# A centred output projection: the second LayerNorm without a mean of its own, and the step loop written out

## The reference

```python
x_inner, z = split(xn @ W_in.T)                 # 512 + 512 channels
x_conv = silu(causal 4-tap depthwise conv(x_inner) + conv_b)
s_C    = (x_conv @ W_x.T)[second half]          # 16 values per token
h_t    = 0.95 * h_{t-1} + x_conv_t              # along the sequence
y      = h * (s_C @ exp(B_log).T) * silu(z)
resid  = xn + y @ W_out.T
attn   = (resid - mean(resid)) * rsqrt(var(resid) + 1e-5) * ln_g + ln_b
ffn    = fp6_blocks(xn) @ fp6_blocks(weight).T + bias   # blocks of 32
out    = x + attn + ffn
```

## Time and profile before

| what | value |
|---|---|
| median of the runs shown | 272.82 us (274.34, 272.82, 272.75) |
| profiled execution, span | 272.2 us, mean granted TensorE clock 0.950 |
| profiled execution, own time | not listed apart from its span; the span is 0.62 us under the median |
| VectorE busy | 236.1 us, 87% |
| TensorE matmul busy | 217.7 us, 80% |
| GpSimd busy | 198.4 us, 73% |
| ScalarE busy | 157.8 us, 58% |

### The profile page before, as it was taken

How to read it: one execution, slowest core, us unless ns; L and a number is a source line. 1 busy time by engine, 2 the same in 40 slices (tenths; PEclk the granted TensorE clock), 3 DMA queues, 4 the chain that set the end, 5 groups by cost and what they waited for, 6 DMA issues and landing times.

```text
span 272.2 us, 3762 instructions
## 1 busy us (share of the span) xinstructions
PE 217.7 (80%) x1252; PEld 180.9 (66%) x1252; DVE 236.1 (87%) x353; ACT 157.8 (58%) x240; POOL 198.4 (73%) x127
## 2 busy tenths in 40 slices
PE   0469959789999997786999895896999988459940
PEld 0348836467898965775898763785989667359930
DVE  4799999989998999689699999689999978785374
ACT  2797773567953456858755355759737263733540
POOL 1428999999568788986586979985697959943142
PEclk9999995979999999999799999999999999959995
DMA  7963000000000000013202000000202000001204
GB/s 234 291 189 125 1 2 0 1 0 0 2 0 1 2 0 1 2 37 117 78 2 77 0 0 0 0 0 0 77 0 77 2 0 0 0 17 64 77 0 154
DMA packets 10773, 11.12 MB, mean 41 GB/s; under 512 B 648, under 2 KB 10120, under 8 KB 10760
## 3 DMA queue, kind: packets, MB, share of 16 engines
q1 hardware_dynamic: 9488, 9.96, 11.1%
q10 hardware_dynamic: 1272, 0.99, 1.3%
HBM read 6.76 MB, written 4.19 MB: 40 GB/s over the span
## 4 chain that ended last, share of the span: by engine, by line
DVE 32%; PE 31%; issue 16%; ACT 11%; POOL 5%; DMA 2%; DVEq 1%; ACTq 0%; POOLq 0%; SPq 0%
DVE hy L1015 6%; DVE xc L986 4%; DVE nmu L1060 4%; PE slot L747 4%; PE slot L749 4%; PE slot L748 4%; PE obank L839 3%; PE obank L838 3%; PE obank L846 3%; DVE hy L1028 3%; POOL hy L407 2%; ACT xn L586 2%; PE obank L749 2%; PE obank L747 2%; PE obank L748 2%
## 5 line engine op out<-in xcount | busy, mean ns | idle before, releaser
L747 PE MATMUL slot<-xn_hi,w_in_lo 128*128 128x512 f32 x128 | 54.9, 429 | 10.2 <-DVE xd_lo L981 4.1
L399 POOL TENSOR_TENSOR xc<-xc,tap 128x1021 f32<-128x1021 f32 x16 | 46.2, 2887 | 14.9 <-DVE xc L986 14.9
L407 POOL TENSOR_TENSOR hy<-hy,sz 128x1024 f32<-128x1024 f32 x16 | 49.6, 3099 | 6.5 <-ACT sz L630 6.5
L749 PE MATMUL slot<-xn_hi,w_in_hi 128*128 128x512 f32 x128 | 53.2, 416 | 0.0
L748 PE MATMUL slot<-xn_lo,w_in_hi 128*128 128x512 f32 x128 | 53.2, 416 | 0.0
L1015 DVE TENSOR_TENSOR_SCAN hy<-decay,xc 128x1024 f32<-128x1024 f32 x16 | 44.0, 2756 | 0.0
L986 DVE SCALAR_TENSOR_TENSOR xc<-slot,cw,xc 128x1023 f32<-128x1023 f32 (+1 forms) x32 | 40.2, 1264 | 2.3 <-ACT tap L623 1.8
L747 PEld LDWEIGHTS slot<-xn_hi,w_in_lo 128*128 128x128 f32 x128 | 25.7, 201 | 21.5 <-DVE xd_lo L981 5.2
L839 PE MATMUL obank<-w_out_hi,y_hi 128*128 128x256 f32 x128 | 32.8, 287 | 0.0
L838 PE MATMUL obank<-w_out_lo,y_hi 128*128 128x256 f32 x128 | 32.6, 285 | 0.0
L749 PEld LDWEIGHTS slot<-xn_hi,w_in_hi 128*128 128x128 f32 x128 | 25.7, 200 | 6.4
(11 more groups left out here) (109 smaller groups left out, 543.0 us busy)
## 6 DMA issues: line engine op xcount, KB each, us to landing
y<-fx SPq DMA_DIRECT2D x7, 512.0 KB, 2.9
x_in<-L_attn_x SPq DMA_DIRECT2D x3, 1024.0 KB, 5.6
x_in<-L_attn_x SPq DMA_DIRECT2D x2, 512.0 KB, 4.1
rs<-L_attn_W_in SPq DMA_DIRECT2D x2, 512.0 KB, 8.9
fx<-L_attn_W_out SPq DMA_DIRECT2D x1, 512.0 KB, 11.7
y<-fx SPq DMA_DIRECT2D x2, 256.0 KB, 2.1
fx<-L_ffn_weight ACTq DMA_DIRECT2D x1, 256.0 KB, 6.8
xc<-L_attn_B_log ACTq DMA_DIRECT2D x1, 256.0 KB
```

Source lines behind the costliest of these rows:

```text
L399: pool.tensor_tensor(xc[:, c, TAPS - 1:], xc[:, c, TAPS - 1:], tap0[:, c % 2, 0:n], ALU.add).then_inc(conv_ready, 1)
L407: pool.tensor_tensor(hy[:, c, :], hy[:, c, :], sz[:, :], ALU.mult).then_inc(hsz_ready, 1)
L747: pe.matmul(dst, w_lo, m_hi, start=first, stop=False)
L749: return pe.matmul(dst, w_hi, m_hi, start=False, stop=last)
```

## The change

- `w_out` is centred on the chip: VectorE sums each of its 512 rows in step -1 (`sum_w_out`), GpSimd divides by 256 and subtracts in step 0 (`centre_w_out`), and `w_out_high` (ScalarE) and `w_out_low` (GpSimd) move from step -1 to step 0, behind it.
- `rs = x * rstd1 + obank` has then the row mean mean1 * rstd1, which is minus `nmr1`, a value that the first LayerNorm has. `nmr1` is kept for three batches, and takes the place of `nmu2`. `mean_2` goes, and so does `accum_out` in `take`.
- `var_2` goes from VectorE. GpSimd adds 256 * eps to the sum of squares, and the factor sqrt(256) goes into the row of ln_g once. `squares` waits for its tile's `take` alone.
- `rstd1_now` and its copy to `rstd1` on GpSimd go; the power is written to `rstd1` itself.
- The loop is written out: all steps are plain instructions with constant semaphore counts.

```diff
         def every_step(step):
-            step(-1); step(0)
-            with eng.Fori(1, LAST) as s:
+            for s in range(-1, NB + 1):
                 step(s)
...
 # GpSimd
-                pool.tensor_tensor(rstd1_now[:, cols], ve1[:, cols], minus_half[:, cols], ALU.pow)
-                wait(pool, xn_ready, NT * (b - 1) + HT * (g + 1))
-                pool.tensor_tensor(nmr1[:, cols], nm1[:, cols], rstd1_now[:, cols], ALU.mult)
-                pool.tensor_copy(rstd1[:, b % XS, cols], rstd1_now[:, cols])
+                pool.tensor_tensor(rstd1[:, b % XS, cols], ve1[:, cols], minus_half[:, cols], ALU.pow)
+                pool.tensor_tensor(nmr1[:, b % XS, cols], nm1[:, cols], rstd1[:, b % XS, cols], ALU.mult)
...
+            def inverse_deviation(cols, b, tiles_done, n):      # rstd_2 and rstd_2_pair
+                wait(pool, sq_done, tiles_done)
+                pool.tensor_scalar(ve2[:, cols], ssq[:, cols], DM * LN_EPS, None, ALU.add)
+                wait(pool, ve2_ready, n)
+                pool.tensor_tensor(rstd2[:, cols], ve2[:, cols], minus_half[...], ALU.pow)
+                wait(pool, rstd2_ready, n)
+                pool.tensor_tensor(nmr2[:, cols], nmr1[:, b % XS, cols], rstd2[:, cols], ALU.mult)
...
+            def centre_w_out():
+                pool.wait_ge(w_sum_ready, 1)
+                pool.tensor_scalar(w_mean[:, :], w_mean[:, :], 1.0 / DM, None, ALU.mult)
+                pool.wait_ge(w_mean_ready, 1)
+                pool.tensor_tensor(w_out_f, w_out_f, w_mean (broadcast over 256), ALU.subtract)
...
+                chain(pool.tensor_scalar(g_row[:, :], g_row[:, :], math.sqrt(DM), None, ALU.mult))  # prepare_bias, step -1
...
 # GpSimd, order of step: scale_g(prev, 0), [centre_w_out, step 0 alone], dequantise(here, 1),
 #   y_low(here, 0), [w_out_low, step 0 alone], y_low(here, 1), y_low(here, 2), rstd_2(prev, 1), ...
...
 # ScalarE
-                wait(act, nmu2_ready, 2 * b + g + 1)
                 for t in range(g * HT, (g + 1) * HT):
+                    wait(act, r_done, NT * b + t + 1)
-                    act.activation(sq_out, rs[:, t, :], ACT.Square, bias=nmu2[:, t:t + 1], accum_out=ssq)
+                    act.activation(sq_out, rs[:, t, :], ACT.Square, bias=nmr1[:, b % XS, t:t + 1], accum_out=ssq)
...
                 xn_high(nxt, 1)
+                if first(here):
+                    w_out_high()
                 y_high(here, 0)
...
 # VectorE
-                dve.scalar_tensor_tensor(rs, x_in, rstd1, obank, ALU.mult, ALU.add, accum_out=rsum)
+                dve.scalar_tensor_tensor(rs, x_in, rstd1, obank, ALU.mult, ALU.add)
-                mean_2(prev, 0)   # and mean_2(prev, 1), var_2(prev, 0), var_2(prev, 1), and both for the pairs
+            def sum_w_out():      # step -1, behind w_ffn_low, ahead of block_inverse(0, 1) and scan(0, 0)
+                dve.wait_ge(w_out_loaded, 16)
+                dve.tensor_reduce(w_mean[:, :], w_out_f, AX.X, ALU.add).then_inc(w_sum_ready, 1)
```

More of the change, by code:

```diff
@@ L27 @@
 from contextlib import ExitStack
+import math
 import numpy as np
@@ L55, in wait @@
 def wait(eng, sem, count):
-    if isinstance(count, int) and count <= 0:
+    if count <= 0:
         return
@@ L112, in build @@
         rstd1 = sb("rstd1", [P, XS, NT])
-        nmr1 = sb("nmr1", [P, NT])
-        rstd1_now = sb("rstd1_now", [P, NT])
+        nmr1 = sb("nmr1", [P, XS, NT])
         xn = sb("xn", [P, NT, DM])
@@ L292, in exists @@
         def exists(b):
-            return not isinstance(b, int) or 0 <= b < NB
+            return 0 <= b < NB
         def first(b):
-            return isinstance(b, int) and b == 0
+            return b == 0
         def of_batch(op):
@@ L305, in is_last @@
         def is_last(b):
-            return isinstance(b, int) and b == LAST
+            return b == LAST
         def of_half(op):
@@ L355, in _ @@
             sp.dma_start(x_in[:, 0, :, :], x_tiles(XS, 0, NT)).then_inc(x_loaded, 16)
-            with sp.Fori(0, LAST) as b:
+            for b in range(LAST):
                 for g in range(2):
@@ L512, in step @@
                 y_low(here, 0)
+                if first(here):
+                    w_out_low()
                 y_low(here, 1)
@@ L518, in step @@
                 conv_tap0(nxt, 1)
-                if first(nxt):
-                    w_out_low()
                 gate(nxt, 0)
-            every_step(pool, step)
+            every_step(step)
             rstd_2_pair(0)
@@ L568, in w_x_and_out_high, with w_out_high @@
                     act.activation(w_x_t[:, :, i * NS:(i + 1) * NS], w_x_f[:, :, NS:2 * NS], ACT.Copy).then_inc(w_x_ready, 1)
-                act.wait_ge(w_out_loaded, 16)
+            def w_out_high():
+                act.wait_ge(w_out_centred, 1)
                 act.activation(w_out_hi[:, :, :], w_out_f, ACT.Copy).then_inc(w_out_hi_ready, 1)
@@ L722, in step @@
                 taps(nxt, 2)
-            every_step(act, step)
+            every_step(step)
             squares_pair(0)
@@ L902, in step @@
                 z_half(nxt, 3)
-            every_step(pe, step)
+            every_step(step)
         @block.vector
@@ L917, in token_stats @@
             def token_stats(b, g):
-                if isinstance(b, int) and b == 0:
+                if b == 0:
                     dve.wait_ge(in0_loaded[g], 16)
@@ L1050, in take @@
                 dve.scalar_tensor_tensor(rs[:, t, :], x_in[:, b % XS, t, :], rstd1[:, b % XS, t:t + 1],
-                                         obank[t % 2][:, 0:DM], ALU.mult, ALU.add,
-                                         accum_out=rsum[:, t:t + 1]).then_inc(r_done, 1)
+                                         obank[t % 2][:, 0:DM], ALU.mult, ALU.add).then_inc(r_done, 1)
                 dve.tensor_tensor(fx[:, t, :], obank[t % 2][:, DM:2 * DM], x_in[:, b % XS, t, :],
                                   ALU.add).then_inc(obank_free, 1)
-            @of_half
-            def mean_2(b, g):
-                cols = tiles(g)
-                wait(dve, r_done, NT * b + HT * (g + 1))
-                dve.tensor_scalar(nmu2[:, cols], rsum[:, cols], -1.0 / DM, None, ALU.mult).then_inc(nmu2_ready, 1)
-            @of_half
-            def var_2(b, g):
-                cols = tiles(g)
-                wait(dve, sq_done, NT * b + HT * (g + 1))
-                dve.tensor_scalar(ve2[:, cols], ssq[:, cols], 1.0 / DM, LN_EPS, ALU.mult, ALU.add).then_inc(ve2_ready, 1)
             @of_batch
@@ L1142, in step @@
                 s_low(here)
-                var_2(prev, 0)
                 take_tile(prev, 4)
@@ L1162, in step @@
                 xd_low(here, 0)
-                mean_2(prev, 1)
                 block_max(nxt, 1)
@@ L1172, in step @@
                 conv_tap2(nxt, 0)
-                var_2(prev, 1)
                 conv_tap1(nxt, 0)
@@ L1180, in step @@
                     w_ffn_low()
+                    sum_w_out()
                 block_inverse(nxt, 1)
```

72 lines of the change are left out of this document (28 added, 44 removed).

## The result

The changed kernel took 265.31 us in the median of four runs (264.35 to 267.32), the kernel before 273.58 us beside it. The ratio is 0.9683, with an interval of 0.9634 to 0.9731: 3.2% faster. The forecast was 264.2 us, also a ratio of 0.968 to the 272.82 us that it started from. The profiled execution took 264.35 us with a span of 262.5 us, 9.7 us under the span before. The two medians are 8.3 us apart. The spans are of one execution each, and eight executions of the changed kernel have spans from 262.5 to 265.4 us (see e11), so the 9.7 carries that spread. Executions more than 1.5% above the fastest of their kernel are left out of all comparisons, three of ten in e1 and two of seventeen of the kernel before beside e5 to e8.

The account below looks back on a forecast made before the run. Bound: VectorE and GpSimd taking turns, with two `mean_2` waits a step. Sum: 0.4 + 2.6 - 6.0 - 2.0 - 2.3 - 0.8 - 0.5 = -8.6 us, span 263.6, plus 0.6 gives 264.2 us; range 260 to 271.

Parts of the forecast that it names:

- step 0, centring: GpSimd's divide and subtract delay ScalarE's `w_out_high` and `y_high(0)`; first output tile 2.6 us later, bounds 1.5 and 5.
- last step with a batch: Both `mean_2` removed there: 0.9 us at `s_low` and 1.1 us between the two `xd_low`, together 2.0 us less.
- end: Behind the last `take`, without the last `mean_2`, VectorE is bound by its own work: 2.3 us less.
- The second wait: `mean_2` between the two `xd_low` of a loop step; removing it gives 1.7 us a step, bounds 0 and 2.4.
- The first wait: `mean_2` behind the scan in mid-step; removing it gives 1.3 us a loop step, bounds 0 to 2.29.
- The clock: A warm TensorE behind the shorter idle, worth up to 1.4 us more in the second step; not in the sum.
- The loop: Writing it out saves hops such as GpSimd's 0.23 us idle: 0 to 2.5 us over two steps, 0.5 taken.
- Accumulator, `var_2`, copy: Dropping accumulator reads in `take`: 0.8 us less; `var_2` counted inside the 1.3 us; GpSimd's addition replaces the copy.
- A: Rival: the gate is served ahead of `quantise(1)`, so `s_low` starts no sooner; 268.9 us, chance 0.12.
- B: Rival: `block_scale` misses the gap between two `y_low`, so `xd_low(here, 1)` stays put; 268.7 us, chance 0.08.
- D: Rival: fetching the written-out code stalls TensorE, some 4 fetches of 2.9 us; slower, 275.8 us, chance 0.08.
- my sign for D: TensorE showing idle time without a releaser in the trace after would mean stalls from fetching the written-out code.

Follow-up runs that it names:

- e11: The changed kernel run and profiled again, not a character changed: 266.18 us, ratio 0.9725 to the kernel before.
- e1: The kernel before with only the step loop written out: 274.10 us, ratio 1.0003 to the kernel before.
- e5: The changed kernel with only the first `mean_2` of a step put back: 272.68 us, ratio 0.9929 to the kernel before.
- e8: The changed kernel without centring, accumulator back, `mean_2` still off VectorE (mean formed on GpSimd): 263.79 us, ratio 0.9629 to the kernel before.
- e3: The changed kernel with a `mean_2` in every old place, as a copy of `nmr1`: 277.63 us, ratio 1.0134 to the kernel before.
- e4: The kernel before with `mean_2` as a reduction over a length-one axis, division left out (timing only): 266.02 us, ratio 0.9696.
- e6: The changed kernel with only the second `mean_2` of a step put back: 269.65 us, ratio 0.9856 to the kernel before.
- e7: The changed kernel with ScalarE's `w_out_high` moved behind `y_high(0)`, `y_high(1)` and `xd_high(0)`: 265.73 us, ratio 0.9701 to the kernel before.
- e2: The changed kernel with the hardware loop back, 256 * eps added from a row of constants: 268.32 us, ratio 0.9774 to the kernel before.
- e9: The version without centring, with ScalarE's `norm_2(prev, 0)` moved behind the two `xn_high(nxt)`: 264.81 us, ratio 0.9695 to the kernel before.

## Why the prediction was right

The sum was -8.6 us. The spans of the two profiled executions show -9.7, the medians -8.3. By its terms:

| step of the prediction | forecast, us | measured, us |
|---|---|---|
| step -1 | +0.4 | +0.1 |
| step 0, centring | +2.6 | +1.9 (e8 gives 2.35 back) |
| step 1 | -3.0 | -4.3 |
| step 2 | -3.0 | -3.2 |
| last step with a batch | -2.0 | -2.0 |
| end | -2.3 | -2.2 |
| accumulator; loop | -0.8; -0.5 | in the rows above; alone, 0 for the loop (e1) |

- **The mechanism**, small instructions that wait for GpSimd's turn, held. e3 and e4 show it from both sides. `s_low` came 1.76 us closer to the scan (1.7 forecast), the second gate 1.57 (1.5), and `xd_low(here, 0)` 1.78 (1.3).
- **The second wait** was forecast at 1.7 us. The distance between the two `xd_low` shrank by 2.34, and alone (e6) the wait costs 2.2 to 2.3, with a fall of the clock in each step. The first wait alone (e5) costs 2.7 to 2.8 where 1.3 was forecast, 1.6 of them without the clock.
- **The clock**, left out of the sum at "up to 1.4 us", goes with what step 1 won beyond step 2: the row went from 0.61 to 1.00, and 4.3 - 3.2 = 1.1 us. This is the mis-sized term by the profiled executions. I had taken the fall as a part of the second step, but it is not tied to it: the third step of the kernel before has the same idle and the full clock, and e11 has a fall where the first profile has none. So these 1.1 us, which are also what the spans show beyond the forecast, may be the luck of two executions.
- **Centring**: the size was 0.7 us too high, and its path was half of what is there. ScalarE's queue, where I put it, is what TensorE waits for (1.98 us), but e7 shows that GpSimd's own added instructions hold the first tile as long by themselves.
- **The loop**: 0.5 us forecast, nothing alone (e1), and beside the other edits (e2) 4.3 us by the spans and 1.3 to 2.5 us by the ratios. Only the 0.4 us a step of longer hops are seen as its own; the rest goes through the clock, which I had not counted, so my bound of 2.5 us is neither shown nor refuted.
- **Accumulator, `var_2`, copy**: 0.5 us for all together by one execution each (e3 against e1), which is within their spread. The 0.8 us that I had given to the accumulator are neither shown nor refuted.
- **The rivals.** A did not come: `quantise(1)` took 1.22 us. B did not: `block_scale` took 0.72 us and TensorE did not wait. But e9 shows B's mechanism as real, 1.29 us when the turn is missed. D did not: 4 packets more, and no stall that they explain. By its letter my sign for D did appear, an idle of 4.49 us without a releaser in step 0, but it ends with ScalarE's `silu` (47.05 against 46.96), and the kernel before has such an idle of 0.59 us at the same place (46.94).
- **From span to time**: I added 0.6 us, the distance from the span of one execution to the median of others. Each run takes 1.8 to 1.9 us more than its own span, so the sum asks for 265.4 to 265.5 us and not 264.2, and measured are 265.31.

That the total came out well owes something to luck, to errors of both signs: the two waits and the clock gave more than forecast and centring cost less, while the 1.3 us of the loop and the accumulator are not seen as gains of their own.

## What to carry to other kernels

Sort the groups of instructions by mean duration against size. A 128x4 operation of 1.7 us was a wait for a turn between VectorE and GpSimd here, and the cheapest cure was another form of the same operation: a reduction over an axis of one (ratio 0.9696) did as well as the whole change (0.9683). The division that it leaves out must then go elsewhere; e8 does this on ScalarE and GpSimd, off the chain of waits. When such a wait stands ahead of TensorE, price what a fall of the clock behind the idle can cost as well (up to 1.4 us a time here), and run the same code twice before reading a difference of that size in one step. When work moves between engines, follow the queue of each of them, since two paths can be equally late.

## What the runs showed of the hardware that was not expected

- The same idle of TensorE, 1.85 and 1.86 us in the same place of the same code, was followed by the full clock in one execution and by 0.53 in another (e11), at 1.4 us a time. So was an idle of 2.06 and 2.07 us in two steps of one execution of the kernel before. What decides it was not settled.
- The addition of a constant on GpSimd (128x4) takes 0.23 to 0.25 us where nothing is in its way, and 562 ns in the mean over its nine places after the change (two of them 128x2); one of them, behind a scan, takes 2.20 us:

```profile
L431 POOL TENSOR_SCALAR ve<-ssq 128x4 f32<-128x4 f32 (+1 forms) x9 | 5.1, 562 | 13.1 <-ACT sq_out L668 9.3 <-ACT sq_out L675 3.7
```

- The subtraction with a broadcast operand (128x1024) took 1.90 us on GpSimd, where the gate and `y_low`, with two full operands, take 2.4.
